# Splitting one progress counter of an LSTM step into several, and moving four tiny vector operations together, in a residual LSTM on one core

## The chip, the cores and the metric

The kernel runs on one core of one Trainium2 chip. The metric is the device time of one execution in microseconds (us). Names used below: PE is TensorE (matrix multiply), PEld its weight loads, DVE is VectorE, ACT is ScalarE, POOL is GpSimd, SP is SyncE (here it issues the DMAs). A "q" behind an engine's name (DVEq) marks an instruction that the engine's sequencer executes by itself: register arithmetic, a branch, a bare wait.

## The reference

`x` is 32 x 512 x 512 (batch B, time T, features D), float32. An LSTM with 512 hidden units runs over T and its hidden states are added to `x`:

```python
xW = jnp.einsum('ntd,dg->ntg', x, Wx) + b          # Wx: 512 x 2048
def step(carry, xw_t):
    prev_h, prev_c = carry
    a = xw_t + prev_h @ Wh                          # Wh: 512 x 2048
    i, f, o = sigmoid(a[:, :Hd]), sigmoid(a[:, Hd:2*Hd]), sigmoid(a[:, 2*Hd:3*Hd])
    g = tanh(a[:, 3*Hd:])
    next_c = f * prev_c + i * g
    next_h = o * tanh(next_c)
    return (next_h, next_c), next_h
return x + hs                                       # h0 = cond_1024, c0 = 0
```

The 512 steps depend on each other through `prev_h @ Wh`; `x @ Wx` does not depend on them.

## The kernel before, in words

Everything is laid out on 128 partitions as 4 column groups of the hidden size times 32 batch rows. A product in near-float32 precision is made of float16 matmuls: each operand is scaled and cut into a high and a low part, and high x high, high x low and low x high are added. The products `x @ Wx` are made for two time steps at once with seven block products in place of eight (buffers `run`, `extra`, `p5`), and are ready in the PSUM banks `Z[0..3]` before the recurrent part of the step is added to them.

**Blocks and loops.** Four time steps (`s` = 0 to 3) make one block `n` of 128. DVE, ACT, SP and POOL run the blocks through `run_blocks`: `body(i)` holds blocks 2i and 2i+1; `body(0)` stands written out, then `Fori(1, 61)` loops over i = 1 to 60 on the engine, then three bodies stand written out. Line 258 is that loop. PE has a loop of its own over single blocks (line 425). Each engine has its own instruction stream; they are ordered by counters (semaphores) that instructions raise when they end and that `wait_ge` waits for. In the loops the value waited for depends on the loop's variable, so the sequencer computes it in a register first.

**One step `t`.** PE adds `h @ Wh` to `Z[s]`: 12 groups of four matmuls side by side. It begins when the first half of `hT_hi` is there (line 754), goes on with its second half, and ends with `hT_lo` (line 794). Between two such parts PE works through 21 shorter groups of `x @ Wx` for later steps, which need `x_lo` (line 619) and a few copies of ACT. ACT then does, for half 0 and half 1 of the columns, sigmoid of i and f (line 500) and tanh of g (line 502), then sigmoid of o (line 505), and later tanh(c) for each half (line 509). DVE does f·c (line 760) and i·g (line 762) of half 0, their sum (line 766), the products of half 1 (line 771), the high part of h for half 0 (line 749), the sum of half 1 (line 775), the transposition of half 0 (line 754), the same for half 1, then h (789), its low part (791), its transposition (794) and the output (801).

**The counters that the change touches.** Before, all seven ACT instructions of a step raise one counter, `gates_done`, and the DVE waits for `7t + 1`, `+2`, `+4`, `+6`, `+7`. The three products raise `igfc_done`, and the sums wait for `3t + 2` and `3t + 3`. Each of these DVE instructions has one wait.

**The scale of a block.** At `s == 3` of block n the DVE computes the power-of-two scales of block n+3 with four instructions on one to four elements per partition, each of which waits for the one before it: `xfield` (632), `xfield_n` (637), `zs` (642), `scales` (650). Before, they are spread: 632 between 794 and 801, 637 and 642 between 801 and 619, 650 after 619. The last of the four has two waits (646 and 649). ACT uses the scales one block later (448), POOL waits for them before its next reduction. At `s == 2` the DVE copies one scale into `h_scale` (661) and waits for that.

Of the kernel before, what the change touches and what calls it, by code (L numbers as in the profile page):

```python
# [10 lines left out]
ALU = mybir.AluOpType  # L11
ACT = mybir.ActivationFunctionType
# [3 lines left out]
def lstm_residual(nc, x, h0, Wx, Wh, bias, out):  # L16
# [20 lines left out]
    NB = T // TB  # L37
# [12 lines left out]
    with ctx:  # L50
        def sb(name, shape, dt=F32):
            return ctx.enter_context(nc.sbuf_tensor(name, shape, dt))
# [4 lines left out]
        def sem(name):  # L57
            return ctx.enter_context(nc.semaphore(name))
# [27 lines left out]
        act = sb("act", [P, ZW])  # L86

        gc = sb("gc", [P, 2, 2, C // 2])
        igfc = sb("igfc", [P, 2, 2, C // 2])
        tanh_c = sb("tanh_c", [P, C])  # L90
# [94 lines left out]
        c22_set = sem("c22_set")  # L185

        z_done = sem("z_done")

        gates_done = sem("gates_done")

        igfc_done = sem("igfc_done")
        c_done = sem("c_done")
        h_hi_done = sem("h_hi_done")
        hT_hi_done = sem("hT_hi_done")
        h32_done = sem("h32_done")
# [16 lines left out]
        def half(tile, a):  # L212
            return tile[:, a * HC:(a + 1) * HC]

        def half_gates(tile, a):
            return tile.rearrange("p (g a c) -> p a g c", g=4, a=2)[:, a]
# [29 lines left out]
        def started(value):  # L246
            return not isinstance(value, int) or value > 0

        def within(value, end):
            return not isinstance(value, int) or value < end  # L250
# [180 lines left out]
        def _(sc):  # L431
# [64 lines left out]
            def step(t, n, s):  # L496
                scale = 1.0 if isinstance(t, int) and t == 0 else z_unscale
                sc.wait_ge(z_done, t + 1)
                for a in range(2):
                    nc.scalar.activation(half_gates(act, a)[:, 0:2], half_gates(Z[s], a)[:, 0:2],  # L500
                                         ACT.Sigmoid, scale=scale).then_inc(gates_done, 1)
                    nc.scalar.activation(gc[:, a, 0], half_gates(Z[s], a)[:, 3],  # L502
                                         ACT.Tanh, scale=scale).then_inc(gates_done, 1)

                nc.scalar.activation(act[:, 2 * C:3 * C], Z[s][:, 2 * C:3 * C],
                                     ACT.Sigmoid, scale=scale).then_inc(gates_done, 1)
                for a in range(2):
                    sc.wait_ge(c_done, 2 * t + 1 + a)
                    nc.scalar.activation(half(tanh_c, a), gc[:, a, 1], ACT.Tanh).then_inc(gates_done, 1)  # L509

            sum_of_x(0, 0, 1)
            sum_of_x(1, 1, 1)
# [82 lines left out]
        def _(v):  # L595
# [31 lines left out]
                v.wait_ge(c21_set, q)  # L627
                nc.vector.tensor_tensor(Z[2 * e + 1][:, HW:], run[e][:, 0:HW], p5[:, :], ALU.add).then_inc(c22_set, 1)

            def field_of_sum(n):  # L630
                v.wait_ge(xmax_shared, n + 1)
                nc.vector.tensor_scalar(xfield[:, :], xmax_all[:, :].bitcast(I32), 255 << MANT, None,
                                        ALU.bitwise_and).then_inc(xfield_done, 1)

            def negate_field(n):
                v.wait_ge(xfield_done, n + 1)
                nc.vector.tensor_scalar(xfield_n[:, :], xfield[:, :], float(LOW_FIELD << MANT), -1.0,
                                        ALU.max, ALU.mult).then_inc(xfield_n_done, 1)

            def scale_of_z(n):  # L640
                v.wait_ge(xfield_n_done, n + 1)
                nc.vector.tensor_scalar(zs[:, :], xfield_n[:, :], zs_of_x[:, :], zs_of_h[:, :],
                                        ALU.add, ALU.min).then_inc(zs_done, 1)

            def scales_of_block(n, r):
                v.wait_ge(zs_done, n + 1)
                if started(n - 1):

                    v.wait_ge(z_unscale_set, n - 1)
                nc.vector.scalar_tensor_tensor(scales[:, r], scale_mul[:, :], zs[:, :], scale_add[:, :],  # L650
                                               ALU.mult, ALU.add).then_inc(scales_done, 1)

            def scale_block(n, r):
                field_of_sum(n)
                negate_field(n)
                scale_of_z(n)
                scales_of_block(n, r)

            def set_h_scale(n, r):
                v.wait_ge(scales_done, n + 1)  # L660
# [84 lines left out]
                scale_block(2, 0)  # L745

            def high_part_of_h(t, a):
                v.wait_ge(gates_done, 7 * t + 6 + a)
                nc.vector.scalar_tensor_tensor(half(h_hi, a), half_gates(act, a)[:, 2], h_scale[:, :], half(tanh_c, a),  # L749
                                               ALU.mult, ALU.mult).then_inc(h_hi_done, 1)  # L750

# [4 lines left out]

            def first_products(t):

                v.wait_ge(gates_done, 7 * t + 1)
                nc.vector.tensor_tensor(igfc[:, 0, 1], half_gates(act, 0)[:, 1], gc[:, 0, 1], ALU.mult).then_inc(igfc_done, 1)  # L760
                v.wait_ge(gates_done, 7 * t + 2)
                nc.vector.tensor_tensor(igfc[:, 0, 0], half_gates(act, 0)[:, 0], gc[:, 0, 0], ALU.mult).then_inc(igfc_done, 1)  # L762

            def first_c(t):
                v.wait_ge(igfc_done, 3 * t + 2)
                nc.vector.tensor_tensor(gc[:, 0, 1], igfc[:, 0, 1], igfc[:, 0, 0], ALU.add).then_inc(c_done, 1)  # L766

            def last_products(t):

                v.wait_ge(gates_done, 7 * t + 4)  # L770
                nc.vector.tensor_tensor(igfc[:, 1], half_gates(act, 1)[:, 0:2], gc[:, 1], ALU.mult).then_inc(igfc_done, 1)

            def last_c(t):
                v.wait_ge(igfc_done, 3 * t + 3)
                nc.vector.tensor_tensor(gc[:, 1, 1], igfc[:, 1, 1], igfc[:, 1, 0], ALU.add).then_inc(c_done, 1)  # L775

            def step(t):
                first_products(t)
                first_c(t)
                last_products(t)  # L780
                high_part_of_h(t, 0)
                last_c(t)
                turn_high_part(t, 0)
                high_part_of_h(t, 1)
                turn_high_part(t, 1)
                if started(t):

                    v.wait_ge(y_done, t)
                nc.vector.tensor_tensor(h32[:, :], act[:, 2 * C:3 * C], tanh_c[:, :], ALU.mult).then_inc(h32_done, 1)
                v.wait_ge(h32_done, t + 1)  # L790
                nc.vector.scalar_tensor_tensor(h_lo[:, :], h32[:, :], h_scale[:, :], h_hi[:, :],  # L791
                                               ALU.mult, ALU.subtract).then_inc(h_lo_done, 1)
                v.wait_ge(h_lo_done, t + 1)
                nc.vector.transpose(hT_lo[:, :, :], h_lo[:, :].rearrange("p (ch l) -> p ch l", ch=NCH)).then_inc(hT_lo_done, 1)  # L794
# [8 lines left out]
            def block(i, n, r):  # L803
                for s in range(TB):
                    step(n * TB + s)
                    if s == 3 and within(n + 3, NB):
                        field_of_sum(n + 3)
                    add_x(i, s, r)
                    if s == 3 and within(n + 3, NB):
                        negate_field(n + 3)  # L810
                    if s == 0:
                        if within(2 * n + 1, NQ):
                            add_extra(2 * n + 1, 1)
                        if within(n + 2, NB):
                            first_forms(n + 2, r)
                    if s == 1:
                        if within(2 * n + 3, NQ):
                            cut_x_lo(2 * n + 3, 1 - r, 1)
                        if within(n + 3, NB):
                            turn_x(n + 3, 1 - r, i + 2 + r)  # L820
                    if s == 2:
                        if within(2 * n + 2, NQ):
                            add_extra(2 * n + 2, 0)
                        if within(n + 2, NB):
                            last_forms(n + 2, r)
                        if within(n + 1, NB):
                            set_h_scale(n + 1, 1 - r)
                    if s == 3:
                        if within(n + 3, NB):
                            scale_of_z(n + 3)  # L830
                        if within(2 * n + 4, NQ):
                            cut_x_lo(2 * n + 4, r, 0)
                        if within(n + 3, NB):
                            scales_of_block(n + 3, 1 - r)

            prepare()
            v.wait_ge(c_cleared, 1)
            run_blocks(v, block)

        @block_ctx.gpsimd  # L840
# [50 lines left out]
```

## Time and profile before

| | |
|---|---|
| median of 3 runs | 2606.32 us (2605.89 to 2606.88) |
| the profiled execution's own time | 2606.32 us |
| its span, from the first to the last instruction | 2604.5 us |
| granted TensorE clock, mean over the span | 0.985 |
| busy: PE, PEld | 2523.2 us (97%), 1811.2 us (70%) |
| busy: DVE, ACT, POOL | 2133.4 us (82%), 1528.4 us (59%), 71.8 us (3%) |
| chain that ended last | PE 96%, DVE 1% |

The profile is of one execution. The remaining 1.8 us between span and time lie around the first and the last instruction. "Busy" is the time in which an engine has at least one instruction under way; matmul ends are modelled. "The chain that ended last" is followed back from the last instruction, at each step to what released it.

### The profile page before, as it was taken

Reading aid. Unit: us, or ns where it says so; the run is one execution under the profiler, and the core shown is the slowest. Engines: PE = TensorE matmul, PEld = TensorE weight load, DVE = VectorE, ACT = ScalarE, POOL = GpSimd, SP = SyncE. Lnnn points to the kernel's source line nnn. Section 1 sums busy time; section 2 is a strip of 40 time slices with the busy share of each in tenths; the row PEclk is TensorE's granted clock in tenths of the full one; section 3 lists DMA queues with packets and bytes.
Section 4 is the critical chain, followed back from the end, with each engine's and each line's share of the span. In section 5 each row is a group of like instructions: output and inputs, shape, how many; then the busy total and the mean of one; then the engine's idle time right before and its main releaser. Section 6 shows DMA issues by size and latency. Waiting matters only on the chain.

```text
span 2604.5 us, 166579 instructions
## 1 busy us (share of the span) xinstructions
PE 2523.2 (97%) x67528; PEld 1811.2 (70%) x67528; DVE 2133.4 (82%) x8771; ACT 1528.4 (59%) x5776; POOL 71.8 (3%) x138
## 2 busy tenths in 40 slices
PE   3599999999999999999999999999999999999998
PEld 0377777777777777777777777777777777777775
DVE  3888888888888888888888888888888888888886
ACT  2556556556656656656656656656656656656654
POOL 3000000000000000000000000000000000000000
PEclk7799999999999999999999999999999999999999
DMA  7011111111111111111111111112111111111111
GB/s 154 18 37 48 37 36 48 36 36 48 36 36 48 36 36 48 36 36 48 36 36 48 36 37 48 36 37 48 36 37 48 36 37 48 36 37 48 36 37 26
DMA packets 223518, 109.86 MB, mean 42 GB/s; under 512 B 25216, under 2 KB 222464, under 8 KB 222464
## 3 DMA queue, kind: packets, MB, share of 16 engines
q1 hardware_dynamic: 223488, 109.48, 16.9%
q8 instruction: 16, 0.26, 0.0%
q14 instruction: 14, 0.11, 0.0%
HBM read 75.83 MB, written 33.55 MB: 42 GB/s over the span
## 4 chain that ended last, share of the span: by engine, by line
PE 96%; DVE 1%; ACT 0%; issue 0%; DVEq 0%; ACTq 0%
PE Z L318 70%; PE run L318 19%; PE extra L318 6%; DVE wh_lo L697 0%; ACT wh_hi L528 0%; DVE h_hi L749 0%; ACT tanh_c L509 0%; DVE x_lo L619 0%; DVE gc L766 0%; ACT act L500 0%; DVE igfc L760 0%; DVE hT_hi L754 0%; DVE igfc L762 0%; ACT forms L448 0%; DVE gc L775 0%
## 5 line engine op out<-in xcount | busy, mean ns | idle before, releaser
L318 PE MATMUL Z<-wh_hi,hT_hi 128*32 128x512 f16 x8176 | 795.8, 379 | 5.1 <-DVE hT_hi L754 5.1
L318 PE MATMUL Z<-wh_lo,hT_hi 128*32 128x512 f16 x8176 | 795.7, 379 | 0.0
L500 ACT ACTIVATE act<-Z 128x128 f32<-128x128 f32 x1024 | 287.7, 281 | 595.1 <-PE Z L318 595.1
L318 PE MATMUL Z<-wh_hi,hT_lo 128*32 128x512 f16 x8176 | 529.8, 379 | 0.0
L318 PE MATMUL run<-wx_hi,x_hi 128*32 128x256 f16 x6120 | 433.6, 273 | 42.5 <-DVE x_lo L619 40.1
L509 ACT ACTIVATE tanh_c<-gc 128x64 f32<-128x64 f32 x1024 | 262.8, 257 | 309.9 <-DVE gc L775 249.2
L318 PE MATMUL run<-wx_lo,x_hi 128*32 128x256 f16 x6120 | 433.7, 273 | 0.0
L318 PE MATMUL run<-wx_hi,x_lo 128*32 128x256 f16 x6120 | 433.7, 273 | 0.0
L318 PE MATMUL Z<-wx_lo,x_hi 128*32 128x256 f16 x6120 | 433.4, 273 | 0.0
L318 PE MATMUL Z<-wx_hi,x_hi 128*32 128x256 f16 x6120 | 433.3, 273 | 0.0
L318 PE MATMUL Z<-wx_hi,x_lo 128*32 128x256 f16 x6120 | 433.3, 273 | 0.0
L749 DVE SCALAR_TENSOR_TENSOR h_hi<-act,h_scale,tanh_c 128x64 f16<-128x64 f32 x1024 | 291.7, 285 | 148.4 <-ACT tanh_c L509 86.3
L318 PEld LDWEIGHTS Z<-wh_hi,hT_lo 128*32 128x32 f16 x8176 | 219.2, 97 | 222.0 <-DVE hT_lo L794 0.7
L318 PEld LDWEIGHTS Z<-wh_hi,hT_hi 128*32 128x32 f16 x8176 | 219.4, 97 | 173.4 <-DVE hT_hi L754 3.7
L318 PEld LDWEIGHTS Z<-wh_lo,hT_hi 128*32 128x32 f16 x8176 | 220.3, 97 | 167.3
L760 DVE TENSOR_TENSOR igfc<-act,gc 128x64 f32<-128x64 f32 x512 | 115.6, 226 | 187.3 <-ACT act L500 187.1
L754 DVE STREAM_TRANSPOSE hT_hi<-h_hi 128x64 f16<-128x64 f16 x1024 | 247.3, 242 | 18.0
L502 ACT ACTIVATE gc<-Z 128x64 f32<-128x64 f32 x1024 | 237.5, 232 | 0.0
L318 PEld LDWEIGHTS run<-wx_hi,x_hi 128*32 128x32 f16 x6120 | 164.3, 97 | 102.1 <-issue 41.0
L458 ACT ACTIVATE x_hi<-forms 128x512 f16<-128x512 f32 x255 | 160.5, 629 | 98.2 <-PE Z L318 98.2
L318 PEld LDWEIGHTS run<-wx_lo,x_hi 128*32 128x32 f16 x6120 | 164.4, 97 | 57.4
L791 DVE SCALAR_TENSOR_TENSOR h_lo<-h,h_scale,h_hi 128x128 f16<-128x128 f32 x512 | 180.2, 352 | 18.1
(89 smaller groups left out, 4047.0 us busy)
## 6 DMA issues: line engine op xcount, KB each, us to landing
x_in<-in_x SPq DMA_DIRECT2D x512, 64.0 KB, 2.1
x_res<-in_x SPq DMA_DIRECT2D x512, 64.0 KB, 2.1
out_y<-y SPq DMA_DIRECT2D x512, 64.0 KB, 1.7
wx_raw<-in_Wx SPq DMA_DIRECT2D x16, 256.0 KB, 9.1
wh_raw<-in_Wh SPq DMA_DIRECT2D x16, 256.0 KB, 20.3
bias_bc<-in_bias SPq DMA_DIRECT2D x4, 64.0 KB, 2.0
h_in<-in_h SPq DMA_DIRECT2D x4, 16.0 KB, 14.3
```

What stands on the lines that cost most here:

```text
L318: return nc.tensor.matmul(out, lhsT, rhs, start=False, stop=last, skip_group_check=True)
L458: nc.scalar.activation(x_hi[:, e], forms_of_pair(r, e), ACT.Copy).then_inc(x_hi_cut, 1)
L500: nc.scalar.activation(half_gates(act, a)[:, 0:2], half_gates(Z[s], a)[:, 0:2], ACT.Sigmoid, scale=scale).then_inc(gates_done, 1)
L502: nc.scalar.activation(gc[:, a, 0], half_gates(Z[s], a)[:, 3], ACT.Tanh, scale=scale).then_inc(gates_done, 1)
L509: nc.scalar.activation(half(tanh_c, a), gc[:, a, 1], ACT.Tanh).then_inc(gates_done, 1)
L749: nc.vector.scalar_tensor_tensor(half(h_hi, a), half_gates(act, a)[:, 2], h_scale[:, :], half(tanh_c, a), ALU.mult, ALU.mult).then_inc(h_h ...
L754: nc.vector.transpose(hT_hi[:, NCH // 2 * a:NCH // 2 * (a + 1), :], half(h_hi, a).rearrange("p (ch l) -> p ch l", l=L)).then_inc(hT_hi_don ...
L760: nc.vector.tensor_tensor(igfc[:, 0, 1], half_gates(act, 0)[:, 1], gc[:, 0, 1], ALU.mult).then_inc(igfc_done, 1)
L791: nc.vector.scalar_tensor_tensor(h_lo[:, :], h32[:, :], h_scale[:, :], h_hi[:, :], ALU.mult, ALU.subtract).then_inc(h_lo_done, 1)
```

## The change

`gates_done` is replaced by four counters (`sig_done` for the sigmoids of i and f, `tanh_g_done`, `sig_o_done`, `tanh_c_done`), and `igfc_done` by three (`fc_done`, `ig_done`, and `igfc_done` for half 1 alone). Three of the DVE's instructions get two waits where they had one. The four functions of the block's scale become one again, `scale_block`, and it is called as a whole at `s == 3`, after `cut_x_lo` (line 619).

```diff
                 for a in range(2):
                     nc.scalar.activation(half_gates(act, a)[:, 0:2], half_gates(Z[s], a)[:, 0:2],
-                                         ACT.Sigmoid, scale=scale).then_inc(gates_done, 1)
+                                         ACT.Sigmoid, scale=scale).then_inc(sig_done, 1)
                     nc.scalar.activation(gc[:, a, 0], half_gates(Z[s], a)[:, 3],
-                                         ACT.Tanh, scale=scale).then_inc(gates_done, 1)
+                                         ACT.Tanh, scale=scale).then_inc(tanh_g_done, 1)
                 nc.scalar.activation(act[:, 2 * C:3 * C], Z[s][:, 2 * C:3 * C],
-                                     ACT.Sigmoid, scale=scale).then_inc(gates_done, 1)
+                                     ACT.Sigmoid, scale=scale).then_inc(sig_o_done, 1)
                 for a in range(2):
                     sc.wait_ge(c_done, 2 * t + 1 + a)
-                    nc.scalar.activation(half(tanh_c, a), gc[:, a, 1], ACT.Tanh).then_inc(gates_done, 1)
+                    nc.scalar.activation(half(tanh_c, a), gc[:, a, 1], ACT.Tanh).then_inc(tanh_c_done, 1)
...
             def high_part_of_h(t, a):
-                v.wait_ge(gates_done, 7 * t + 6 + a)
+                if a == 0:
+                    v.wait_ge(sig_o_done, t + 1)
+                v.wait_ge(tanh_c_done, 2 * t + 1 + a)
...
             def first_products(t):
 
-                v.wait_ge(gates_done, 7 * t + 1)
-                nc.vector.tensor_tensor(igfc[:, 0, 1], half_gates(act, 0)[:, 1], gc[:, 0, 1], ALU.mult).then_inc(igfc_done, 1)
-                v.wait_ge(gates_done, 7 * t + 2)
-                nc.vector.tensor_tensor(igfc[:, 0, 0], half_gates(act, 0)[:, 0], gc[:, 0, 0], ALU.mult).then_inc(igfc_done, 1)
+                v.wait_ge(sig_done, 2 * t + 1)
+                nc.vector.tensor_tensor(igfc[:, 0, 1], half_gates(act, 0)[:, 1], gc[:, 0, 1], ALU.mult).then_inc(fc_done, 1)
+                v.wait_ge(tanh_g_done, 2 * t + 1)
+                nc.vector.tensor_tensor(igfc[:, 0, 0], half_gates(act, 0)[:, 0], gc[:, 0, 0], ALU.mult).then_inc(ig_done, 1)
 
             def first_c(t):
-                v.wait_ge(igfc_done, 3 * t + 2)
+                v.wait_ge(fc_done, t + 1)
+                v.wait_ge(ig_done, t + 1)
...
             def last_products(t):
 
-                v.wait_ge(gates_done, 7 * t + 4)
+                v.wait_ge(sig_done, 2 * t + 2)
+                v.wait_ge(tanh_g_done, 2 * t + 2)
...
             def last_c(t):
-                v.wait_ge(igfc_done, 3 * t + 3)
+                v.wait_ge(igfc_done, t + 1)
...
             def block(i, n, r):
                 for s in range(TB):
                     step(n * TB + s)
-                    if s == 3 and within(n + 3, NB):
-                        field_of_sum(n + 3)
                     add_x(i, s, r)
-                    if s == 3 and within(n + 3, NB):
-                        negate_field(n + 3)
...
                     if s == 3:
-                        if within(n + 3, NB):
-                            scale_of_z(n + 3)
                         if within(2 * n + 4, NQ):
                             cut_x_lo(2 * n + 4, r, 0)
                         if within(n + 3, NB):
-                            scales_of_block(n + 3, 1 - r)
+                            scale_block(n + 3, 1 - r)
```

## Rows read from the trace of the kernel before

**Rows 1.** Busy time by engine, 1000 us of the steady stretch; columns: PE, PEld, DVE, ACT, POOL busy (x instructions), granted clock, DMA share, GB/s
```profile
200.00:1200.00 1000.00, 1000.00 (x27048) 723.74 (x27044) 832.15 (x3483) 602.09 (x2306) 17.89 (x51) 1.00 0.16 40
```

**Rows 2.** Who waited for whom, 200 to 2500 us: total us, times, longest
```profile
DVE igfc L760 <- ACT act L500: 167.2, 471, 0.5
```

**Rows 3.** Timeline, one steady step: start, us, engine, line, operation, operands [idle before]
```profile
1001.19 0.28 ACT L500 ACTIVATE act<-Z 128x128 f32<-128x128 f32 x1 [0.83 <-PE Z L318]
...
1002.78 0.23 DVE L754 STREAM_TRANSPOSE hT_hi<-h_hi 128x64 f16<-128x64 f16 x1
...
1003.26 0.39 PE L318 MATMUL Z<-wh_hi,hT_hi 128*32 128x512 f16 x4
...
1006.07 0.28 ACT L500 ACTIVATE act<-Z 128x128 f32<-128x128 f32 x1 [1.47 <-PE Z L318]
```

**Rows 4.** Timeline, last steps, where PE stands idle before the recurrent part
```profile
2584.70 0.24 DVE L754 STREAM_TRANSPOSE hT_hi<-h_hi 128x64 f16<-128x64 f16 x1
...
2585.00 0.40 PE L318 MATMUL Z<-wh_hi,hT_hi 128*32 128x512 f16 x4 [0.30 <-DVE hT_hi L754]
```

**Rows 5.** Groups by line, DVE, 200 to 2500 us: busy us, mean ns, idle us before
```profile
L791 DVE SCALAR_TENSOR_TENSOR h_lo<-h,h_scale,h_hi 128x128 f16<-128x128 f32 x471 | 165.8, 352 | 16.7
...
L766 DVE TENSOR_TENSOR gc<-igfc 128x64 f32<-128x64 f32 x471 | 105.9, 225 | 16.1
...
L615 DVE TENSOR_TENSOR forms<-forms 128x128 f32<-128x128 f32 x118 | 34.5, 292 | 12.3
```

**Rows 6.** One line's instructions, line 614, 200 to 2500 us: ns min/median/max, first and last start
```profile
L614 DVEq EVENT_SEMAPHORE  x118: 21/21/21, 214.8 to 2499.8; - x118
```

**Rows 7.** Timeline, DVE, from step s=2 into step s=3
```profile
996.24 0.15 DVE L661 COPY h_scale<-scales 128x1 f32<-128x1 f32 x1
996.62 0.23 DVE L760 TENSOR_TENSOR igfc<-act,gc 128x64 f32<-128x64 f32 x1 [0.23 <-ACT act L500]
```

**Rows 8.** Timeline, DVE, end of step s=3 and start of the next, across the loop's end
```profile
999.47 0.31 DVE L794 STREAM_TRANSPOSE hT_lo<-h_lo 128x128 f16<-128x128 f16 x1
...
1000.11 0.27 DVE L642 TENSOR_SCALAR zs<-xfield_n,zs_of_x,zs_of_h 128x1 int32<-128x1 int32 x1
1000.30 0.68 DVE L619 TENSOR_TENSOR x_lo<-forms,x_hi 128x512 f16<-128x512 f32 x1
1000.90 0.22 DVE L650 SCALAR_TENSOR_TENSOR scales<-scale_mul,zs,scale_add 128x4 int32<-128x4 int32 x1
1001.50 0.23 DVE L760 TENSOR_TENSOR igfc<-act,gc 128x64 f32<-128x64 f32 x1 [0.38 <-ACT act L500]
```

**Rows 9.** Timeline, DVE, step s=1: the same tail without the scale's operations
```profile
1009.22 0.31 DVE L794 STREAM_TRANSPOSE hT_lo<-h_lo 128x128 f16<-128x128 f16 x1
1009.46 0.25 DVE L801 TENSOR_TENSOR y<-h,x_res 128x128 f32<-128x128 f32 x1
1009.63 0.68 DVE L619 TENSOR_TENSOR x_lo<-forms,x_hi 128x512 f16<-128x512 f32 x1
```

**Rows 10.** Timeline, DVE, preparation: the four operations in one piece behind line 619
```profile
101.75 0.65 DVE L619 TENSOR_TENSOR x_lo<-forms,x_hi 128x512 f16<-128x512 f32 x1
...
103.00 0.22 DVE L650 SCALAR_TENSOR_TENSOR scales<-scale_mul,zs,scale_add 128x4 int32<-128x4 int32 x1
103.14 0.22 DVE L760 TENSOR_TENSOR igfc<-act,gc 128x64 f32<-128x64 f32 x1
```

**Rows 11.** One line's instructions, line 258 (the loop), 1000.40 to 1000.95 us
```profile
L258 DVEq ALU_OP  x1: 40/40/40, 1000.4 to 1000.4; - x1
L258 DVEq COMPARE_BRANCH  x1: 56/56/56, 1000.5 to 1000.5; - x1
L258 DVEq FUSED_REGOPS  x1: 85/85/85, 1000.8 to 1000.8; - x1
```

**Rows 12.** The same question for 1000.56 to 1000.82 us
```profile
nothing on L258; most used: ['L318', 'L619', 'L308']
```

**Rows 13.** Line 258 over the whole span
```profile
L258 DVEq COMPARE_BRANCH  x60: 50/56/67, 180.2 to 2484.8; - x60
```

More of the change, by code:

```diff
@@ L187, in lstm_residual @@
         z_done = sem("z_done")
-        gates_done = sem("gates_done")
+        sig_done = sem("sig_done")
+        sig_o_done = sem("sig_o_done")
+        tanh_g_done = sem("tanh_g_done")
+        fc_done = sem("fc_done")
+        ig_done = sem("ig_done")
         igfc_done = sem("igfc_done")
         c_done = sem("c_done")
+        tanh_c_done = sem("tanh_c_done")
         h_hi_done = sem("h_hi_done")
@@ L628, in add_extra, with scale_block @@
                 nc.vector.tensor_tensor(Z[2 * e + 1][:, HW:], run[e][:, 0:HW], p5[:, :], ALU.add).then_inc(c22_set, 1)
-            def field_of_sum(n):
+            def scale_block(n, r):
                 v.wait_ge(xmax_shared, n + 1)
@@ L633, in field_of_sum @@
                                         ALU.bitwise_and).then_inc(xfield_done, 1)
-            def negate_field(n):
                 v.wait_ge(xfield_done, n + 1)
@@ L638, in negate_field @@
                                         ALU.max, ALU.mult).then_inc(xfield_n_done, 1)
-            def scale_of_z(n):
                 v.wait_ge(xfield_n_done, n + 1)
@@ L643, in scale_of_z @@
                                         ALU.add, ALU.min).then_inc(zs_done, 1)
-            def scales_of_block(n, r):
                 v.wait_ge(zs_done, n + 1)
@@ L651, in scales_of_block @@
                                                ALU.mult, ALU.add).then_inc(scales_done, 1)
[L653 to L657, printed above, removed]
             def set_h_scale(n, r):
```

## The prediction

> **What bounds the kernel now.** I read the busy times by stage first. In 1000 us of the steady stretch PE is busy for 1000.00 us at the full granted clock [rows 1], so its order of matmuls sets the time: one step from ACT's first sigmoid to the next takes 1006.07 - 1001.19 = 4.88 us [rows 3]. The list of waits of 200 to 2500 us has no row at all in which PE waits; the DVE waits 471 times for the first sigmoid, 167.2 us in all, a mean of 0.35 us per step [rows 2]. So the change can't make the steady part faster. It can only make it slower, by eating the slack with which h reaches PE.
>
> How large is that slack? In the steady step the first half of `hT_hi` ends at 1002.78 + 0.23 = 1003.01 and the first matmul on it starts at 1003.26, 0.24 to 0.25 us later; I take 0.24 [rows 3]. In the last steps PE is idle and waits for it: there the transposition ends at 2584.94 and the matmul starts at 2585.00, 0.06 later [rows 4]. What PE does not need of the 0.24 is **the slack: 0.18 us per step**. The last transposition (line 794) hangs on the same chain and shifts with it.
>
> **The change, part by part.**
>
> *Counters.* ACT raises another counter from the same instruction: nothing. A DVE instruction with one wait starts right behind what it waits for: line 791 after 789 with 16.7/471 = 0.035 us of idle, line 766 with 16.1/471 = 0.034 [rows 5]. With two waits the trace shows one as an instruction of its own: of line 615's two, the one written last (line 614) is an EVENT_SEMAPHORE of 21 ns [rows 6], and line 615, which waits through it for the instruction in front, starts 12.3/118 = 0.104 us behind it [rows 5]. The sequencer stands at the bare wait, and only then hands on the instruction behind it. So **a bare wait that is the last to be fulfilled costs 0.104 - 0.035 = 0.07 us**.
>
> Three instructions get a second wait. Line 766: `ig_done` is written last and is the one fulfilled last, +0.07. Line 771: `tanh_g_done` of half 1 has long been fulfilled; it is covered by line 766's execution, 0. Line 749 for half 0: `tanh_c_done` is written last and fulfilled last, +0.07 (the trace has no bare wait of the DVE for ACT; I take the same value; bounds 0 and, should a bare wait plus a scalar_tensor_tensor cost more than a tensor_tensor, 0.10). Line 749 of half 1, 760, 762 and 775 keep one wait. The two lie in series on the way to both transpositions, so h arrives **0.13 to 0.14 us later in every step**; I use 0.13. That alone is below 0.18: 0.05 us are left and PE doesn't stall. This is why I don't charge 512 steps with it.
>
> The Trainium skill says otherwise: "VectorE: DVE Perf Modes", section "The DRAIN you can't avoid", holds that the semaphore costs nothing extra between chained vector operations. For a wait carried by the instruction the trace's 0.035 us leaves room for that; for a bare wait the 0.104 us speaks against it. By the page the counters would cost 0 (rival A).
>
> *Step s=3.* Its line 760 comes behind line 661, a wait for it and a register operation. Line 661 ends at 996.39 and line 760 starts at 996.62 [rows 7]. With everything 0.13 later it ends at 996.52; 0.035 for the wait, about 0.046 for a register operation (estimate from the 40 to 85 ns of [rows 11]) and 0.05 to hand on the next instruction (0.07 less the 0.021 of the bare wait) make 996.65: 0.03 late. Its h is then 0.16 late, still under 0.18.
>
> *The four operations moved.* They now run in a row behind line 619, after the loop's last big operation. From line 794 to 801 it is 0.24 us and from 801 to 619 0.17 [rows 9]. From 619 to 650 it is 103.00 - 101.75 = 1.25 [rows 10], and 0.03 more since 619 takes 0.68 in the loop. With line 794 at 999.47 [rows 8] and 0.16 late, `zs` ends and line 650 may be handed on at 999.47 + 0.16 + 0.24 + 0.17 + 1.28 - 0.03 = 1001.29, in place of 1000.11 + 0.27 = 1000.38 [rows 8]. As work of the engine this still fits: line 760 could start 0.14 behind line 650 [rows 10], at 1001.32 + 0.14 = 1001.46, before 1001.50.
>
> What does not fit is the loop. In the trace the sequencer's loop instructions follow as soon as `zs` has ended (1000.38): the addition at 1000.4, the branch at 1000.5, then nothing from 1000.56 to 1000.82, then the registers of the next iteration, 85 ns [rows 11, 12]. From the end of `zs` to their end: 1000.82 + 0.085 - 1000.38 = **0.525 us, 0.26 of them behind the taken branch**. Before, line 619 still ran then, and line 650 was queued behind it: all of it was covered. After the change the sequencer stands at line 650's wait until 1001.29, goes through the same 0.525 us and hands on line 760 after 0.05 more: 1001.86, against 1001.50 [rows 8]: **0.36 us late**. This step's h is late by 0.36 + 0.13 = 0.49; less 0.18, PE stalls for **0.31 us**. Queued behind line 760 is the whole step; ACT's tanh(c) and PE wait for it.
>
> This happens where the branch is taken: 60 passes [rows 13], 59 of them taken, so 59 x 0.31 = **18.3 us**. Where a block ends within an iteration there is no branch, and a register operation is covered (1001.29 + 0.035 + 0.046 + 0.05 = 1001.42). The last four or five steps, which wait for h, get 0.13 each: 0.6 us. Nothing else pays: `x_lo` comes 0.3 us earlier, but PE reads it a block's step later and never waits for it; ACT reads the scales more than 2 us later; SP and POOL have a block's time.
>
> Sum against the profiled execution, whose time of 2606.32 is the median too: 2606.3 + 18.3 + 0.6 = **2625 us**, +0.7%.
>
> **The rivals.** 0.2% (5.2 us) is about what a measurement of this kernel can tell from no change.
>
> A. *Bare waits are free, no change.* With 0 in place of 0.07, line 794 is not late, `zs` ends at 1001.13, line 760 starts at 1001.70, 0.20 late, and the stall is 0.02 x 59 = 1 us: 2607.5. For it: a bare wait takes only 21 ns. Against: the 0.104 us of line 615, a mean over 118. With one of the two costs the stall is 0.20 + 0.07 + 0.07 - 0.18 = 0.16, 59 of them 9.4 us: 2616.
>
> B. *The branch stays covered, no change.* If the sequencer could go past line 650's wait and branch while line 650 waits, line 760 would be on time, the 0.18 us would hold the 0.13, and the time would be 2607. For it: line 650 is started 0.5 us after its wait was fulfilled, so there is a queue behind the sequencer. Against: the loop's addition comes right at the end of `zs`, and not before [rows 8, 11]. It decides once h of that step is later than 0.18.
>
> C. *Every step stalls.* If a bare wait on ACT costs 0.10 or more and line 766's too, h is 0.20 late in each step: 0.02 x 450 = 9 us; at the loop's edge line 760 is 0.36 + 0.07 late, and the stall 0.43 + 0.20 - 0.18 = 0.45, 59 of them 27 us: 2642. For it: a margin of 0.05 us is small and no row shows this wait. Against: nothing in line 766's form differs from line 615's.
>
> D. *Faster.* It needs PE to have waited for something that comes earlier now; `x_lo` does, but no row has PE waiting.
>
> **How the numbers follow.** Forecast (stalls at the loop's edge, +0.35 to +1.2%) 0.70; A and its half-way case below +0.2% 0.07, between +0.2 and +0.35% 0.05; B 0.07; C (above +1.2%) 0.09; D 0.02. Faster by over 0.2% 0.02, within 0.2% 0.14, slower 0.84. The range 2612 to 2638 leaves out A at its end, B, D and the upper part of C, together 0.2; it holds the half-way case of 2616 and half of C's excess.
>
> **What the profile after would show.** Line 766's idle goes from 0.034 to about 0.10 us, and line 749's start moves by 0.13 against line 500. PE's first matmul on `hT_hi` starts 2.07 us behind line 500 in seven of eight steps, as now, and 2.38 in the eighth. The waits list PE (or its loads) for `hT_hi` 59 times, about 0.3 us each; line 258's register operation stands behind line 650, and line 760 0.36 us later than now. The DVE is less idle before 760. It would be wrong if the compiler placed the other of the two waits on its own, if the registers of the loop's head took longer or shorter, or if a matmul whose weights come late loses more than the 0.06 us that the idle PE shows.

## The result and the profile after

The changed kernel takes 2628.23 us (median of 4 runs, 2627.37 to 2629.15), the kernel before 2606.6 (4 runs, 2605.89 to 2607.86): a ratio of 1.0083, 95% interval 1.0065 to 1.0100. That is 21.6 us more; 2625 was forecast, with a range of 2612 to 2638. The profiled execution took 2627.08 us, its span is 2625.3 us at a granted clock of 0.987. In the new file the lines are 503 for 500, 512 for 509, 742 for 749, 747 for 754, 753 and 755 for 760 and 762, 760 for 766, 766 for 771, 770 for 775, 786 for 791, 789 for 794, 796 for 801, 622 for 619, 618 for 615, 635, 638, 641 and 647 for the four scale operations, 321 for 318 (the matmuls) and 261 for the loop.

Who waited for whom, 200 to 2500 us of the changed kernel (total us, times, longest):

```profile
PEld Z L321 <- DVE hT_lo L789: 94.7, 467, 0.2
...
DVE igfc L753 <- ACT act L503: 78.5, 292, 0.4
PEld Z L321 <- DVE hT_hi L747: 56.3, 234, 0.4
```

Before, no row of PE or of its weight loads stood here. A weight load that waits is not yet a matmul that waits: in the trace of before the load of the first matmul on `hT_hi` starts at 1003.15, 0.11 us ahead of its matmul at 1003.26 [rows 3], so most of these 151 us are hidden. They show that the slack is nearly used up, and the longest one, 0.4 us, is where it is exceeded. The row of `hT_hi` has 234 waits where the prediction expected 59 of 0.3 us: the steps s=3 and the second half of `hT_hi` are in it too. The DVE has lost half its own: line 753 waits for ACT for 78.5 us where it was 167.2 [rows 2].

Groups by line, DVE, same stretch (busy us, mean ns | idle us before):

```profile
L786 DVE SCALAR_TENSOR_TENSOR h_lo<-h,h_scale,h_hi 128x128 f16<-128x128 f32 x467 | 164.4, 352 | 16.5
...
L760 DVE TENSOR_TENSOR gc<-igfc 128x64 f32<-128x64 f32 x467 | 105.2, 225 | 48.5
...
L618 DVE TENSOR_TENSOR forms<-forms 128x128 f32<-128x128 f32 x116 | 34.0, 293 | 12.1
```

Line 760, which now stands behind a bare wait, is idle for 48.5/467 = 0.104 us where it was 0.034 [rows 5]: the very value of line 618 (12.1/116 = 0.104), from which it was forecast. Line 786 keeps 0.035.

Timeline, the end of the last block of an iteration and the step behind it:

```profile
967.32 0.31 DVE L789 STREAM_TRANSPOSE hT_lo<-h_lo 128x128 f16<-128x128 f16 x1
967.55 0.25 DVE L796 TENSOR_TENSOR y<-h,x_res 128x128 f32<-128x128 f32 x1
967.73 0.68 DVE L622 TENSOR_TENSOR x_lo<-forms,x_hi 128x512 f16<-128x512 f32 x1
968.32 0.15 DVE L635 TENSOR_SCALAR xfield<-xmax_all 128x1 int32<-128x1 int32 x1
...
968.69 0.27 DVE L641 TENSOR_SCALAR zs<-xfield_n,zs_of_x,zs_of_h 128x1 int32<-128x1 int32 x1
968.87 0.28 ACT L503 ACTIVATE act<-Z 128x128 f32<-128x128 f32 x1 [0.83 <-PE Z L321]
969.00 0.22 DVE L647 SCALAR_TENSOR_TENSOR scales<-scale_mul,zs,scale_add 128x4 int32<-128x4 int32 x1
...
969.54 0.23 DVE L753 TENSOR_TENSOR igfc<-act,gc 128x64 f32<-128x64 f32 x1 [0.31 <-ACT act L503]
...
970.26 0.26 ACT L512 ACTIVATE tanh_c<-gc 128x64 f32<-128x64 f32 x1 [0.54 <-DVE gc L760]
...
970.62 0.29 DVE L742 SCALAR_TENSOR_TENSOR h_hi<-act,h_scale,tanh_c 128x64 f16<-128x64 f32 x1 [0.15 <-ACT tanh_c L512]
...
970.96 0.24 DVE L747 STREAM_TRANSPOSE hT_hi<-h_hi 128x64 f16<-128x64 f16 x1
...
971.25 0.10 PEld L321 LDWEIGHTS Z<-wh_hi,hT_hi 128*32 128x32 f16 x4 [0.42 <-DVE hT_hi L747]
971.25 0.40 PE L321 MATMUL Z<-wh_hi,hT_hi 128*32 128x512 f16 x4
...
974.08 0.28 ACT L503 ACTIVATE act<-Z 128x128 f32<-128x128 f32 x1 [1.29 <-PE Z L321]
```

The row of the same line that begins the next step:

```profile
978.96 0.28 ACT L503 ACTIVATE act<-Z 128x128 f32<-128x128 f32 x1 [0.83 <-PE Z L321]
```

And line 261's instructions, 968.9 to 969.6 us (ns min/median/max, first and last start), and the same question for 969.15 to 969.40:

```profile
L261 DVEq ALU_OP  x1: 40/40/40, 969.0 to 969.0; - x1
L261 DVEq COMPARE_BRANCH  x1: 56/56/56, 969.1 to 969.1; - x1
L261 DVEq FUSED_REGOPS  x1: 85/85/85, 969.4 to 969.4; - x1
```

```profile
nothing on L261; most used: ['L321', 'L503', 'L505', 'L311', 'L647']
```

ACT's tanh(c) and the DVE operation that waits for it, in a normal step of before:

```profile
1002.15 0.26 ACT L509 ACTIVATE tanh_c<-gc 128x64 f32<-128x64 f32 x1
...
1002.44 0.28 DVE L749 SCALAR_TENSOR_TENSOR h_hi<-act,h_scale,tanh_c 128x64 f16<-128x64 f32 x1
```

Read them together. In a normal step line 753 starts 0.31 us behind ACT's first sigmoid [rows 3, 8: 1001.50 - 1001.19]; here it is 969.54 - 968.87 = 0.67, so 0.36 late. The list blames ACT, as releasers go by semaphores, but ACT's sigmoid had ended at 969.15. What was late is the sequencer: `zs` ends at 968.96, the loop's addition starts at 969.0, the branch at 969.1, nothing runs until 969.4, and the loop head's registers end at 969.49, 0.05 before line 753. The first matmul on `hT_hi` starts 971.25 - 968.87 = 2.38 us behind the sigmoid, as forecast. The step from 968.87 to 974.08 is 5.21 us, the next one 4.88: 0.33 us lost; the mean over the trace is 0.323. 59 such steps make 19 us of the 21.6.

The second bare wait stands in front of line 742: it starts 970.62 - 970.52 = 0.10 us behind the end of ACT's tanh(c), where line 749 started 1002.44 - 1002.41 = 0.03 behind it.

### The profile page after: what moved, and what is told of

Its sections match the earlier page's. It is cut to its first block, busy times and chain, and to the rows that moved or that the text cites. A ratio compares the mean times of both kernels' runs of the same rounds, so it can differ in the third digit from the quotient of the medians.

```text
span 2625.3 us, 164755 instructions
## 1 busy us (share of the span) xinstructions
PE 2534.0 (97%) x67528; PEld 1769.6 (67%) x67528; DVE 2176.8 (83%) x8771; ACT 1528.8 (58%) x5776; POOL 72.4 (3%) x138
## 4 chain that ended last, share of the span: by engine, by line
PE 68%; DVE 20%; issue 4%; ACT 4%; DVEq 1%; ACTq 0%
PE Z L321 53%; PE run L321 12%; PE extra L321 4%; DVE h_hi L742 3%; ACT tanh_c L512 3%; DVE h_lo L786 2%; DVE gc L760 2%; DVE igfc L755 2%; DVE hT_hi L747 2%; DVE x_lo L622 1%; DVE y L796 1%; DVE gc L770 1%; DVE igfc L753 1%; DVE h L784 1%; DVE Z L628 1%
```

## The experiments

Runs of one group shared their chip and their runs of the kernel before: its median was 2607.16 us in the first group (e1 to e4), 2606.77 in the second (e5 to e7), and 2606.09 in the third (e9, e10).

**e1, the move alone.** On the kernel before:

```diff
-                    if s == 3 and within(n + 3, NB):
-                        field_of_sum(n + 3)
                     add_x(i, s, r)
...
-                            scales_of_block(n + 3, 1 - r)
+                            scale_block(n + 3, 1 - r)
```

(and without the calls of `negate_field` and `scale_of_z`).

> The kernel before with one part of the change: the four scale operations in one piece behind line 619, the counters left as they were. Theory (the branch is uncovered and two bare waits add 0.13 us to h, both needed): line 760 behind the loop's edge is about 0.20 to 0.23 us late, just over the slack of 0.18, so the stall is 0.02 to 0.05 us at 59 edges: 2608 to 2610 us. Rival (the move alone costs it all, the counters are free): 2626 to 2628.

Measured: 2607.11 us, ratio 1.0001 (0.9991 to 1.0010), a little under what was expected. The move alone costs nothing that can be told. In its trace line 760 is 0.18 us late behind a taken branch, not 0.20 to 0.23, so the slack just holds it, and these steps are 0.01 us longer. Its list of waits shows how near it comes: the weight loads wait 58 times, once per taken branch in the stretch.

```profile
PEld Z L318 <- DVE hT_hi L754: 10.5, 58, 0.2
```

**e2, the counters alone.** The changed kernel with the four operations spread as before:

```diff
                     step(n * TB + s)
+                    if s == 3 and within(n + 3, NB):
+                        field_of_sum(n + 3)
                     add_x(i, s, r)
...
-                            scale_block(n + 3, 1 - r)
+                            scales_of_block(n + 3, 1 - r)
```

(and with the calls of `negate_field` and `scale_of_z` at their old places).

> The changed kernel with the scale operations spread out again as before: the counters alone. Theory: h reaches PE 0.13 to 0.14 us later in every step, which is under the slack of 0.18, so no stall but 0.006 us in step s=3 and 0.8 us in the last steps: 2607 to 2609 us. Rival (the counters cost by themselves, in every step): 2620 or more.

Measured: 2609.04 us, ratio 1.0009 (1.0000 to 1.0019), at the edge of what can be told from no change. Its loads wait in every step, 0.2 us at most, and nearly all of it is hidden:

```profile
PEld Z L321 <- DVE hT_lo L801: 92.8, 471, 0.2
```

So of the two parts one costs 0 and the other about 2 us, and both together 21.6. The loss is not a sum; it comes from two delays that share one slack.

**e3, the two waits in the other order.** The changed kernel with

```diff
-                v.wait_ge(fc_done, t + 1)
                 v.wait_ge(ig_done, t + 1)
+                v.wait_ge(fc_done, t + 1)
...
-                if a == 0:
-                    v.wait_ge(sig_o_done, t + 1)
                 v.wait_ge(tanh_c_done, 2 * t + 1 + a)
+                if a == 0:
+                    v.wait_ge(sig_o_done, t + 1)
```

> The changed kernel with the two waits of line 760 (the sum of half 0) and of line 742 (high part of h, half 0) written in the other order, so that the one fulfilled long before becomes the bare wait. Same instructions, same counters, same place of the scale operations. Theory: no delay of h, the edge's stall falls from 0.323 to about 0.03 us: 2608 to 2610 us, 18 us less than the changed kernel. Rival (a second wait costs whichever it is, or the waits don't matter): 2626 to 2628.

Measured: 2606.34 us, ratio 1.0000 (0.9990 to 1.0009). Nothing else differs, and the whole loss is gone, even the 2 us that were expected to stay (the edge is that of e1). Line 760 starts as it did before the change, although a bare wait of 21 ns still stands in front of it. It is still line 759, the wait written last, but this is now the one for `fc_done`, which is fulfilled early:

```profile
L760 DVE TENSOR_TENSOR gc<-igfc 128x64 f32<-128x64 f32 x471 | 105.9, 225 | 16.1
```

```profile
L759 DVEq EVENT_SEMAPHORE  x471: 21/21/21, 200.5 to 2495.8; - x157
```

16.1/471 = 0.034 us. Line 742 starts 0.034 us behind the end of tanh(c), a mean over the stretch, where it was 0.102. It is not the number of waits that costs, but whether the bare one is the last to be fulfilled.

**e4, one of the two swapped.** Only the first hunk of e3 (lines 758 and 759).

> The changed kernel with only line 760's two waits swapped; line 742 still stands behind a bare wait for tanh(c). Theory: the delay per step is halved to 0.065 us, it counts twice at the edge (once in the step before, once in the step behind), and 0.03 us of step s=3 goes: the stall is 0.323 - 0.131 - 0.03 = 0.16 us, 59 times 9.6 us: 2616 to 2618 us. Rival (one of the two waits alone carries it): 2609 or 2626.

Measured: 2617.26 us, ratio 1.0040 (1.0025 to 1.0054): 10.1 us over its kernel before, half the loss, as the count of delays says (one bare wait counts twice at the loop's edge). The one that is left is the wait for ACT: line 742 still starts 0.102 us behind tanh(c).

**e5, the scale in front of `x_lo`.** The changed kernel with

```diff
-                        if within(2 * n + 4, NQ):
-                            cut_x_lo(2 * n + 4, r, 0)
                         if within(n + 3, NB):
                             scale_block(n + 3, 1 - r)
+                        if within(2 * n + 4, NQ):
+                            cut_x_lo(2 * n + 4, r, 0)
```

> The changed kernel with scale_block in front of cut_x_lo at s=3 in place of behind it: the same instructions, still in one piece, but the 0.68 us of line 622 runs while the sequencer branches. Theory: line 753 is on time at the loop's edge, the delay of 0.13 us stays under the slack: 2607 to 2609 us. Rival (four dependent operations in a row cost by their latency, wherever they stand): 2620 or more.

Measured: 2609.05 us, ratio 1.0008 (0.9998 to 1.0017): that of e2. The four dependent operations stand in one piece here too; their latency is not the cost. The last long operation has to run while the sequencer branches.

**e6, a loop of four blocks.** The changed kernel with

```diff
-            with engine.Fori(1, last - 3) as i:
-                body(i)
+            with engine.Fori(0, 30) as m:
+                body(m * 2 + 1)
+                body(m * 2 + 2)
```

> The changed kernel with loops of four blocks in place of two on DVE, ACT, SP and POOL (30 iterations, 29 taken branches in place of 59). The order of all work is the same. The loop's head has one more register operation, about 0.06 us. Theory: half as many stalls of 0.32 to 0.39 us, 9.4 to 11.3 us: 2617 to 2620 us. Rival (the loss comes with every block, 120 times, not with the branch): 2626 to 2628. If the longer loop's branch has to fetch more: over 2621.

Measured: 2728.72 us, ratio 1.0462 (1.0444 to 1.0479): neither theory, but the third case named, and by far more than was thought. Line 261 in its trace, 1046 to 1050 us, and the DVE's timeline there:

```profile
L261 DVEq COMPARE_BRANCH  x1: 63/63/63, 1046.7 to 1046.7; - x1
...
L261 SPq COMPARE_BRANCH  x1: 45/45/45, 1047.3 to 1047.3; - x1
L261 SPq FUSED_REGOPS  x1: 74/74/74, 1047.6 to 1047.6; - x1
L261 DVEq FUSED_REGOPS  x1: 98/98/98, 1049.8 to 1049.8; - x1
```

```profile
1046.59 0.22 DVE L648 SCALAR_TENSOR_TENSOR scales<-scale_mul,zs,scale_add 128x4 int32<-128x4 int32 x1
1050.04 0.22 DVE L754 TENSOR_TENSOR igfc<-act,gc 128x64 f32<-128x64 f32 x1 [3.23 <-issue]
```

The same branch takes 3.1 us in place of 0.3 (2.8 to 3.9 over the 29) once the DVE's loop body is twice as long; nothing else in the DVE's code differs but a register operation of the loop's head. PE is idle behind each of the 29; its row in the list of waits, 200 to 2600 us:

```profile
PE Z L322 <- DVE hT_hi L748: 86.2, 29, 3.8
```

That is 86 of the 122 us lost. Another 16 us are the clock: behind nine of the 29 stalls the granted clock falls to 1.2 GHz for a few microseconds. At 475.75, behind a stall of 3.76 us, a matmul on `hT_hi` takes 0.64 us in place of 0.39, and this step takes 11.4 us where one behind a stall without such a fall takes about 8. Between 200 and 2500 us the trace of the changed kernel has no such fall, and none of its stalls is longer than 0.4 us. Some 13 us more lie in other steps, most of them as 0.13 to 0.16 us in two steps per iteration, and weren't taken apart. As a test of the number of edges the run says nothing; e9 takes its place.

**e7, a third bare wait.** On e2, `v.wait_ge(c_cleared, 1)` in front of the wait for `sig_done` in `first_products`.

> The kernel with the counters alone and a third bare wait on the chain: line 760 of the kernel before (the first product) gets a wait that was fulfilled at the start, written before that for the sigmoid, so that the sigmoid's becomes the bare one. h is 0.20 us late in every step. Theory: of the slack of 0.18 us 0.044 were left with two; the third (0.065) exceeds it by 0.02 us, in step s=3 by 0.07: 8 + 9 = 17 us, 2622 to 2628 us, and PE waits in every step. Rival (late weights hide behind the matmul under way, or the slack is larger): 2607 to 2610.

Measured: 2618.98 us, ratio 1.0041 (1.0026 to 1.0055), but not by the mechanism meant. The register operation that computes the value for `sig_done` took up the wait for `c_cleared`, so that of `sig_done` stayed on its instruction, and no third delay arose in the loop. Much of the time was lost elsewhere: in one step of each iteration the sum of half 0 comes 0.21 us behind its product, 0.10 more than in all others,

```profile
997.37 0.22 DVE L768 TENSOR_TENSOR igfc<-act,gc 128x64 f32<-128x64 f32 x1
997.80 0.23 DVE L773 TENSOR_TENSOR gc<-igfc 128x64 f32<-128x64 f32 x1 [0.21 <-DVE igfc L768]
```

59 times in the stretch. This step is 0.07 us longer and the one behind it 0.04: 6.6 of the 12.2 us. The bare wait in front of line 773 is executed on time, at 997.63, and the sum starts 0.17 us behind it in place of 0.065. Why there, and where the rest went, was not tried further. As a test of the slack it is inconclusive; e10 replaces it.

**e9, half the edges.** The changed kernel with 30 of its 60 looped bodies written out:

```diff
-            with engine.Fori(1, last - 3) as i:
+            with engine.Fori(1, last - 33) as i:
                 body(i)
-            for i in range(last - 3, last):
+            for i in range(last - 33, last):
                 body(i)
```

> The changed kernel with the same loop body of two blocks, but 30 iterations in the loop (29 taken branches) and the other 30 bodies written out behind it, on DVE, ACT, SP and POOL. Theory: the stall of 0.323 us comes 29 times, 9.4 us in place of 19.1; with 1.5 us of the rest 2617 to 2619 us. Rival (the loss belongs to the block's end, not to the branch): 2626 to 2628.

Measured: 2625.18 us, ratio 1.0070 (1.0053 to 1.0087): 19.1 us over its kernel before, 2.5 us less than the changed kernel's 21.6 where 9 to 10 were expected. Line 752 in its trace and in that of the changed kernel tells a part of why:

```profile
L752 DVEq EVENT_SEMAPHORE  x68: 21/21/21, 102.9 to 2596.9; - x68
```

```profile
L752 DVEq EVENT_SEMAPHORE  x8: 21/21/21, 102.8 to 2598.6; - x8
```

In written-out code there is no register operation between the wait for `h_scale_set` and that for the sigmoid, so the sigmoid's becomes a bare wait in each step s=3: 60 more, which lengthen these steps by about 0.03 us (2 us in all). Some single steps there are 0.1 to 0.4 us longer with nothing before them that the profile names, 2.7 us together. And the very first step, before any branch, takes 9.1 us in this trace and 6.6 in that of the changed kernel. It differs without order between traces (6.4 in that of e3, 9.1 in that of e2). Why, for both, stays open. The direct count is better than this run's total: its loop holds 29 branches, and the steps of 0.32 us too much stand behind each of these, not behind the block ends in between. They cost 9.6 us in the trace where the changed kernel's 59 cost 19.1.

**e10, a doubled wait.** On e2, `v.wait_ge(sig_done, 2 * t + 1)` written twice. Both have the same value, no register operation comes between them, and one becomes bare.

> The kernel with the counters alone, and line 766 (the first product; line 753 of the changed kernel) waits for the same value of sig_done twice, so that one of the two is a bare wait fulfilled last: a third 0.065 us on the chain, in every step. Theory: with two bare waits the matmul still starts 0.10 us behind the transposition where 0.056 would do, a reserve of 0.044; the third exceeds it by 0.02 us in each of 480 steps, somewhat more at s=3: 10 to 15 us on top of the 2609 of the counters alone, 2618 to 2624 us. Rival (more reserve than the idle PE shows): 2607 to 2610.

Measured: 2637.71 us, ratio 1.0118 (1.0101 to 1.0134). Timeline of a normal step:

```profile
1002.75 0.28 ACT L503 ACTIVATE act<-Z 128x128 f32<-128x128 f32 x1 [0.87 <-PE Z L321]
...
1004.55 0.24 DVE L759 STREAM_TRANSPOSE hT_hi<-h_hi 128x64 f16<-128x64 f16 x1
...
1004.85 0.40 PE L321 MATMUL Z<-wh_hi,hT_hi 128*32 128x512 f16 x4
...
1007.67 0.28 ACT L503 ACTIVATE act<-Z 128x128 f32<-128x128 f32 x1 [1.29 <-PE Z L321]
```

The matmul now starts 1004.85 - 1004.79 = 0.06 us behind the transposition, the value of the idle PE [rows 4], and the step is 4.92 us. So the slack is what rows 3 and 4 said, and past it every nanosecond counts. The cost was expected too small, 10 to 15 us where it is 28.7 over e2 (29.7 if each is taken over its own kernel before), and the time lies outside 2618 to 2624: 0.037 us per step in place of 0.02 (0.01 of it is a slower start of the first matmuls once they had to wait, and the reserve was a little under 0.01 smaller), and 0.11 in each s=3 rather than 0.07. These steps are the cleanest measure: h is 0.075 us later in them than in the others, and they are 0.075 us longer.

## Why the prediction was right, step by step

- *The bound and the slack.* Right: 0.18 us per step. e10 crosses it and the matmul stands at 0.06 us behind the transposition; e2 stays below it.
- *A bare wait fulfilled last costs 0.07 us.* Right: 0.104 against 0.034 us at line 760. It holds also for ACT's tanh(c), of which no row of before spoke: 0.102 against 0.033 us at line 742. e3 takes both away by order alone, e4 one, for all and half of the loss.
- *Step s=3, 0.03 us late, no stall.* Slightly too small: line 753 is 0.04 us later there, h 0.18, which is just the slack, and each such step is 0.006 us longer. In e2's trace these steps carry 0.7 us and the last steps 0.9 (0.6 forecast), of a loss of about 2 us; its loads wait for `hT_hi` 120 times, about once per block.
- *The loop's edge.* Right in mechanism and size: from the end of `zs` to the end of the loop head's registers 0.53 us (0.525 forecast), line 753 0.36 us late (0.36), the first matmul on `hT_hi` 0.31 (0.31), the step 0.32 longer. e1, e2 and e5 show that each of its three ingredients is needed: the late waits, the scale operations at the very end, and no long operation behind them.
- *59 x 0.31 + 0.6 = 18.9 us* against 21.6 measured. Of the 20.8 us between the two profiled executions, the edges are 59 x 0.323 = 19.1 (the 0.01 beyond 0.31 is the slower start of the first matmuls that e10 shows too), the steps s=3 are 0.8, for which nothing was forecast, and the last steps 0.9. The other 0.8 us lie between profiled executions and medians.
- *Rival A* fell. The rule of the Trainium skill beside it ("VectorE: DVE Perf Modes", section "The DRAIN you can't avoid": the semaphore costs nothing extra) holds for a wait carried by the instruction (0.034 us, e3) and fails for a bare one fulfilled last. *Rival B* (the branch covered) fell with the rows of line 261 after. *Rival C* (a stall in each step) needs one bare wait more, as e10 shows. *Rival A's* own case is e3: its stall at the edge is 0.01 us, where 0.02 was thought. *Rival D* fell: nothing is faster.

No version beat the kernel before: e3 and e1 equal it, since PE sets its time.

## What to carry to other kernels

Where the bound engine has a small slack per step, add up all delays against that one slack before calling any of them free: the late waits alone (e2) and the late branch alone (e1) cost 0.1% and nothing, both together 0.8%. With two waits on one instruction, write first the one that is fulfilled last (here the one written last becomes the bare wait), and keep a long operation with early waits as the last thing before a loop's branch. In these traces the sequencer doesn't branch before the last wait is fulfilled: the loop's addition starts at 969.0, `zs` ends at 968.96, and before the change they stood at 1000.4 and 1000.38.

## What the runs showed of the hardware that was not expected

- A taken branch of the DVE costs 0.32 us from its start to the next instruction with a body of two blocks, and 3.1 us with one of four (e6), while the same loop's branch on SP goes only from 0.16 to 0.28 us. What the chip does in these 3 us the trace doesn't say. The Trainium skill ("Runtime: NRT & Kernel Launch", section "Instruction fetch mechanics") says that a branch to a target outside the sequencer's window of two pages has to wait for a fetch; e6 fits that, and no run here shows the window's size.
- In e7 a delay of 0.10 us stands once per iteration between a bare wait and the sum behind it, always at the same instruction. That a bare wait only makes visible what is otherwise covered is a guess: no run tests it.
